# Product G's two outermost steps on half of the array's rows each, and where its results are read

## The chip, the cores and the metric

One core of one Trainium2 chip runs the whole program. The metric is the device time of one execution in microseconds (us).

## The reference, cut to what matters

Four layers, each `x = x + ffn(cond(x, style))` on x of 32 x 64 x 1024. `cond` is four modulated convolutions in a row over the 1024 positions of each of the 32 batches, with 64 channels in and out and 3 taps: the same length, up by 2 (transposed, then a blur), the same length, and a blur with a step down by 2.

```python
TYPES = ('same', 'upsample', 'same', 'downsample')
out = x
for i, typ in enumerate(TYPES):
    out = _layer(out, style, weights[i], biases[i], mod_w[i], mod_b[i], typ)
```

`_layer` scales the weights by the style of each batch, so each batch has weights of its own. `ffn` differs by layer: a product in fp8 (layer 0), a product with a low-rank top-2 of 16 experts (1), with 8 experts under a sparsemax (2), and a gated product of low rank (3).

## The kernel before, in words

The 32 batches are taken as 16 pairs (`NP` = 16). In a pair, h = 0 or 1 is the batch. A batch's 64 channels fill half of the 128 partitions, its even and odd positions the two halves, so a matmul has 128 rows. Every fp32 value is split in a high and a low part, and every product is three matmuls (`PASSES`: high by high, low by high, high by low).

Convolutions 2 to 4 of a batch are multiplied into one set of weights before they meet the data. For each pair there are, on TensorE (PE in the profile):

- `weights_a` (A, L796): 6 matmuls of 384 columns into bank 2. It waits for `gl_ready`, the reading of the pair before's product G from that bank.
- `weights_g` (G, L815): for each batch five steps e = -2 to 2 of three matmuls, 128 x 256 each, 30 in all. The window of 256 columns moves by 64 from step to step. Batch 0's result is in bank 2, batch 1's in bank 0. In the outermost steps half of the 128 rows have weights that are zero. `g_done` rises after each batch's 15 matmuls.
- `conv0` (L784): the first convolution, 12 matmuls of 512 columns into banks 0 and 1.
- `main` (L832): G's result by conv0's, 24 matmuls of 512 columns into banks 3 and 4.
- `transpose_h` (L841): 8 transposes of the result, into the same banks.
- `ffn` (L861, L877, L885 or L856), in layers 1 to 3 only. Layer 0's fp8 product is a stage of its own behind its 16 pairs.

Every engine has its order written out by hand, and semaphores tie them. ScalarE (ACT) reads a result from a bank and writes its high part, VectorE (DVE) reads it again and writes the low part: `read_u` (L968, L1124) for conv0, `read_g` (L973, L1130) for G, `read_a` (L962, L1118) for A, and `split_h` for the transposes. In layer 0 split_h is `H_all` on ACT (L989) and then `hmax`, a maximum over the pair, on DVE (L1141), whose end raises `hl_ready`. GpSimd (POOL) patches the edges of main's result before the transposes (L119).

`over_pairs` runs p = 0 (`first`), a loop over p = 1 to 12, and p = 13, 14, 15. `ahead` says how many pairs still follow. In iteration p, PE does A(p + 1), main(p), conv0(p + 1), transposes(p), G(p + 1), and in layers 1 to 3 ffn(p). So in layer 0, G(p + 1) is followed by A(p + 2) and main(p + 1), which open iteration p + 1.

```python
for h in range(2):
    pe.wait_ge(gl_ready, 2 * (g0 + p) + h + 1)
    pe.wait_ge(ul_ready, 2 * (g0 + p) + h + 1)
    if h == 0:
        wait_pos(pe, hh_ready, g0 + p)
        wait_pos(pe, hl_ready, g0 + p)
```

So main of a pair waits, before its first matmul, for its own G's low part (`gl_ready`) and for the split_h of the pair before (`hh_ready`, `hl_ready`), whose banks it writes again.

In p = 0 the order is another one, in all layers: A(1), edges_p, main(0), edges_v, conv0(1), edges_y, G(1), transposes(0), then ffn(0). The edge pass (`edges_u`, `edges_p`, `edges_v`, `edges_y`) computes the few positions at the ends of all batches. Its second product, `edges_p` (L743), has 64 rows: 9 matmuls of batch 0 on partitions 0 to 63, then 9 of batch 1 on partitions 64 to 127. Its results go through a long chain on DVE (L1178 to L1153) before `edges_v` (L756). G(0) stands ahead of p = 0.

## Time and profile before

| | |
|---|---|
| median of 3 runs | 2453.69 us (2453.54 to 2454.59) |
| the profiled execution | 2454.0 us, its span 2452.2 us |
| mean granted TensorE clock | 0.949 of full speed |
| PE busy | 2157.9 us, 88% |
| PE weight loads busy | 1796.4 us, 73% |
| DVE, ACT, POOL busy | 1093.3, 781.7, 447.8 us |
| G's matmuls (L815) | 1920, three groups of 640, 282 to 290 ns each |

The span is the time from the first to the last instruction of the profiled execution. Matmuls overlap, so one that lasts 0.28 us is followed by the next 0.12 us after its start; what a product takes is read from the starts.

### The profile page before, as it was taken

How to read it: one execution, taken by the hardware profiler on the slowest of the kernel's cores; microseconds unless marked ns; L12 is line 12 of the kernel's file. 1: busy time of each engine (PE TensorE's matmuls, PEld its weight loads, DVE VectorE, ACT ScalarE, POOL GpSimd, SP SyncE). 2: the span in 40 equal slices, each digit the busy share in tenths (PEclk: the TensorE clock that was granted, in tenths of full speed). 3: DMA queues.
4: the chain of work that ended last, by engine and by line, in shares of the span. 5: the costliest groups of instructions: out<-in, count | busy, mean ns of one | idle time of the engine just before them, and what ended most of it. 6: DMA issues, size and time to landing. Idle time of an engine off the chain costs nothing. (4 is left out here: it accounts for less than half of the span.)

```text
span 2452.2 us, 32019 instructions
## 1 busy us (share of the span) xinstructions
PE 2157.9 (88%) x10900; PEld 1796.4 (73%) x10900; DVE 1093.3 (45%) x1992; ACT 781.7 (32%) x1294; POOL 447.8 (18%) x478
## 2 busy tenths in 40 slices
PE   2799956679999995997599999997999979987997
PEld 2688832568888884886488888886888958866885
DVE  4656669634444433232443344435444424433442
ACT  2255621223323321011322232312454434423441
POOL 4021125320100110000411111111000012342334
PEclk9899989889999997998799999998999989998999
DMA  5333224322111203224211111102010021132123
GB/s 140 112 94 94 78 86 171 129 69 70 59 51 60 68 35 132 86 86 131 87 52 51 51 60 58 62 35 72 26 34 26 25 65 45 45 109 82 51 59 120
DMA packets 99008, 182.01 MB, mean 74 GB/s; under 512 B 21232, under 2 KB 50928, under 8 KB 98544
## 3 DMA queue, kind: packets, MB, share of 16 engines
q1 hardware_dynamic: 97680, 179.40, 23.2%
q10 hardware_dynamic: 1280, 1.97, 0.4%
q8 instruction: 30, 0.49, 0.1%
q14 instruction: 18, 0.15, 0.0%
HBM read 127.27 MB, written 46.92 MB: 71 GB/s over the span
## 5 line engine op out<-in xcount | busy, mean ns | idle before, releaser
L832 PE MATMUL ps<-l_u_hi,l_g_hi 128*128 128x512 f32 x512 | 205.1, 401 | 0.0
L832 PE MATMUL ps<-l_u_lo,l_g_hi 128*128 128x512 f32 x512 | 202.6, 396 | 0.0
L832 PE MATMUL ps<-l_u_hi,l_g_lo 128*128 128x512 f32 x512 | 202.6, 396 | 0.0
L1124 DVE TENSOR_TENSOR l_u_lo<-ps,l_u_hi 128x512 fp32r<-128x512 f32 x128 | 88.5, 693 | 222.3 <-ACT l_u_hi L968 222.2
L815 PE MATMUL ps<-l_a_hi,c_hi 128*128 128x256 f32 x640 | 185.8, 290 | 0.0
L815 PE MATMUL ps<-l_a_hi,c_lo 128*128 128x256 f32 x640 | 180.5, 282 | 0.0
L815 PE MATMUL ps<-l_a_lo,c_hi 128*128 128x256 f32 x640 | 180.3, 282 | 0.0
L119 POOL TENSOR_TENSOR l_hs<-l_EY,ones 128x4 f32<-128x4 f32 x128 | 28.2, 221 | 789.8 <-ACT l_hs L979 789.6
L877 PE MATMUL ps<-l_w_hi,l_h_hi 128*128 128x512 f32 x512 | 167.3, 408 | 0.0
L877 PE MATMUL ps<-l_w_lo,l_h_hi 128*128 128x512 f32 x512 | 163.4, 400 | 0.0
L877 PE MATMUL ps<-l_w_hi,l_h_lo 128*128 128x512 f32 x512 | 162.9, 399 | 0.0
L2047 POOL TENSOR_TENSOR f_a_lo<-f_prod,f_a_hi 128x512 fp32r<-128x512 f32 (+1 forms) x88 | 113.5, 1290 | 268.9 <-ACT f_a_hi L1950 268.9
L1874 PE MATMUL ps<-pt_hi,f_v_hi 128*128 128x512 f32 (+1 forms) x352 | 139.6, 397 | 25.3 <-DVE f_v_lo L1988 25.3
L784 PE MATMUL ps<-l_x_hi,c_hi 128*128 128x512 f32 x256 | 105.5, 412 | 63.1 <-DVE l_x_lo L1103 63.1
L979 ACT ACTIVATE l_hs<-ps,l_EY,dem3e 128x512 f32<-128x512 f32 x128 | 99.0, 777 | 156.0 <-PE ps L832 141.8
L2003 DVE SCALAR_TENSOR_TENSOR f_prod<-ps,f_b,f_gate 128x512 f32<-128x512 f32 (+1 forms) x88 | 66.0, 750 | 179.0 <-ACT f_gate L1943 179.0
L1874 PE MATMUL ps<-pt_lo,f_v_hi 128*128 128x512 f32 (+1 forms) x352 | 140.4, 399 | 0.0
L1874 PE MATMUL ps<-pt_hi,f_v_lo 128*128 128x512 f32 (+1 forms) x352 | 140.3, 398 | 0.0
L1130 DVE SCALAR_TENSOR_TENSOR l_g_lo<-ps,s_u,l_g_hi 128x512 fp32r<-128x512 f32 x128 | 95.8, 751 | 94.9 <-ACT l_g_hi L973 93.9
L962 ACT ACTIVATE l_a_hi<-ps,s_p 128x256 fp32r<-128x256 f32 x128 | 53.7, 470 | 252.6 <-PE ps L796 252.6
L973 ACT ACTIVATE l_g_hi<-ps,s_u 128x512 fp32r<-128x512 f32 x128 | 87.9, 688 | 122.7 <-PE ps L815 122.7
L968 ACT ACTIVATE l_u_hi<-ps 128x512 fp32r<-128x512 f32 x128 | 76.8, 600 | 143.2 <-PE ps L784 143.2
(303 smaller groups left out, 5073.8 us busy)
## 6 DMA issues: line engine op xcount, KB each, us to landing
xin<-x SPq DMA_DIRECT2D x96, 256.0 KB, 4.0
l_xr<-x SPq DMA_DIRECT2D x32, 512.0 KB, 4.5
x<-l_xr SPq DMA_DIRECT2D x32, 512.0 KB, 2.7
l_stage<-in_ffn_w SPq DMA_DIRECT2D x24, 512.0 KB, 3.3
f_v<-in_ffn_v SPq DMA_DIRECT2D x84, 128.0 KB, 2.7
xnat<-in_x SPq DMA_DIRECT2D x16, 512.0 KB, 3.5
xin<-xpl SPq DMA_DIRECT2D x64, 128.0 KB, 2.9
q_xr<-in_x SPq DMA_DIRECT2D x16, 512.0 KB, 3.8
```

The lines of the kernel that those rows point to most:

```text
L784: mm = nc.tensor.matmul(ps[:, h, :], c_part[ws][:, B0 + t * P:B0 + (t + 1) * P], Xs[ms][:, h, t:t + HALF], start=(k == 0), stop=(k == 5))
L815: mm = nc.tensor.matmul(ps[:, bank, at:at + 4 * C], c_part[ws][:, UT + at:UT + at + P], As[ms][:, h, :], start=(k == 0), stop=(k == 14), s ...
L832: mm = nc.tensor.matmul(ps[:, 3 + h, :], Gs[ws][:, h, at:at + P], Us[ms][:, h, 1 + q:1 + q + HALF], start=(k == 0), stop=(k == 11))
L877: mm = nc.tensor.matmul(ps[:, 5 + o, :], hsp[ws][:, b, :], wsp[ms][:, b, o * HALF:(o + 1) * HALF], start=(k == 0), stop=(layer == 1 and k ...
L968: nc.scalar.activation(Us[0][:, h, 1:HALF + 1], ps[:, h, :], ACT.Copy).then_inc(uh_ready, 1)
L973: nc.scalar.activation(Gs[0][:, h, :], ps[:, 2 if h == 0 else 0, :], ACT.Copy, scale=column(s_u, p, h)).then_inc(gh_ready, 1)
L979: nc.scalar.activation(hs[:, h, :], ps[:, 3 + h, :], ACT.Identity, bias=EY[:, 1, 0, bass.ds(h * NP + p, 1)], scale=dem3e[:, bass.ds(h * NP ...
L1124: v.tensor_tensor(Us[1][:, h, 1:HALF + 1], ps[:, h, :], Us[0][:, h, 1:HALF + 1].bitcast(F32), ALU.subtract).then_inc(ul_ready, 1)
L1130: v.scalar_tensor_tensor(Gs[1][:, h, :], ps[:, 2 if h == 0 else 0, :], column(s_u, p, h), Gs[0][:, h, :].bitcast(F32), ALU.mult, ALU.subtr ...
L1874: mm = nc.tensor.matmul(ps[0:m, 2 * g + gu, :], v1sp[ws][:, s, r, gu, 0:m], pt[ms][:, r, cols], start=(k == 0), stop=(k == 5))
L2003: v.scalar_tensor_tensor(prod[0:m, g, :], ps[0:m, 2 * g + 1, :], b1[0:m, 1, bass.ds(2 * i + g, 1)], gate[0:m, g, :], ALU.add, ALU.mult).th ...
L2047: nc.gpsimd.tensor_tensor(asp[1][0:m, g, :], prod[0:m, g, :], asp[0][0:m, g, :].bitcast(F32), ALU.subtract).then_inc(al_ready, 1)
```

## The change

G's 30 matmuls become 18 whole ones (128 rows, the steps e = 1, 0 and -1 of both batches) and 12 with 64 rows (`ends`). The 64-row ones go in pairs: a step of one batch on partitions 0 to 63 and one of the other batch on 64 to 127, which write different banks. The order is now: 6 whole of batch 0, 6 whole of batch 1, 6 halves, 6 whole, a wait for `ends_done`, 6 halves. `g_done` rises by 2 at the very end, where it rose by 1 after each batch. The wait for `ul_ready` stands behind 6 matmuls, where it stood behind 15.

`edges_p` issues its two batches' 64-row matmuls in turn.

In layer 0, and there alone, G(p + 1) stands before the transposes of p on PE, and read_g before split_h on ACT and DVE. In layers 1 to 3 that order stays.

The remaining edits rename semaphores: `side` is shared by layers 1 to 3 with an offset `side0`, and `ends_done` is new. They add or remove no instruction.

```diff
@@ PE: edges_p, the edge pass's second product
-                for h in range(2):
-                    rows = slice(h * C, h * C + C)
-                    k = 0
-                    for t in range(TAPS):
-                        for ws, ms in PASSES:
+                k = 0
+                for t in range(TAPS):
+                    for ws, ms in PASSES:
+                        for h in range(2):
+                            rows = slice(h * C, h * C + C)
                             mm = nc.tensor.matmul(
                                 ps[:, 5 + h, 0:NP * 3 * PW].rearrange("p (n k) -> p n k", k=PW),
                                 c_part[ws][rows, CU + t * P:CU + (t + 1) * P], UEs[ms][rows, :, t:t + PW],
                                 start=(k == 0), stop=(k == 8))
-                            k += 1
+                        k += 1
@@ PE: weights_g, product G
-                for h in range(2):
-                    if h == 0:
-                        pe.wait_ge(al_ready, 2 * (g0 + p) + 2)
-                    else:
-                        pe.wait_ge(ul_ready, 2 * (g0 + p) + 1)
-                    bank = 2 if h == 0 else 0
-                    k = 0
-                    for e in range(-2, 3):
-                        at = (2 - e) * C
-                        for ws, ms in PASSES:
-                            mm = nc.tensor.matmul(ps[:, bank, at:at + 4 * C],
-                                                  c_part[ws][:, UT + at:UT + at + P], As[ms][:, h, :],
-                                                  start=(k == 0), stop=(k == 14), skip_group_check=True)
-                            k += 1
-                    mm.then_inc(g_done, 1)
+                pe.wait_ge(al_ready, 2 * (g0 + p) + 2)
+
+                def window(h, e, rows, ws, ms, **flags):
+                    at = (2 - e) * C
+                    return nc.tensor.matmul(ps[:, 2 if h == 0 else 0, at:at + 4 * C],
+                                            c_part[ws][rows, UT + at:UT + at + P], As[ms][rows, h, :],
+                                            skip_group_check=True, **flags)
+
+                def whole(h, e):
+                    for k, (ws, ms) in enumerate(PASSES):
+                        window(h, e, slice(0, P), ws, ms, start=(e == 1 and k == 0), stop=False)
+
+                def ends(pairs):
+                    for ws, ms in PASSES:
+                        for h, e, rows in pairs:
+                            mm = window(h, e, rows, ws, ms, start=False, stop=(pairs is last_ends and ws == 1))
+                    return mm
+
+                first, second = slice(0, C), slice(C, P)
+                first_ends, last_ends = ((0, 2, first), (1, -2, second)), ((0, -2, second), (1, 2, first))
+                whole(0, 1)
+                whole(0, 0)
+                pe.wait_ge(ul_ready, 2 * (g0 + p) + 1)
+                whole(1, 1)
+                whole(1, 0)
+                ends(first_ends).then_inc(ends_done, 1)
+                whole(0, -1)
+                whole(1, -1)
+                pe.wait_ge(ends_done, g0 + p + 1)
+                ends(last_ends).then_inc(g_done, 2)
@@ PE: iteration
                 main(p)
                 if ahead:
                     conv0(p + 1)
+                if layer == 0 and ahead:
+                    weights_g(p + 1)
                 transpose_h(p)
-                if ahead:
-                    weights_g(p + 1)
                 if layer > 0:
+                    if ahead:
+                        weights_g(p + 1)
                     ffn(p)
@@ ACT and DVE: iteration, the same edit on both
                 if ahead:
                     read_u(p + 1)
+                    if layer == 0:
+                        read_g(p + 1)
                 split_h(p)
-                if ahead:
+                if ahead and layer > 0:
                     read_g(p + 1)
```

What PE issues in a late iteration of layer 0, before. L784 is conv0, L841 a transpose, L815 G, L796 A, ident and l_hs the operands of a transpose, gl_ready the low part of G.

```order
L841 MATMUL ps<-ident,l_hs 128x128 [waits hs_patched]
L841 MATMUL ps<-ident,l_hs 128x128 x3
L841 MATMUL ps<-ident,l_hs 128x128 [waits hs_patched]
L841 MATMUL ps<-ident,l_hs 128x128 x3
L815 MATMUL ps<-l_a_hi,c_hi 128x256 [waits al_ready]
L815 MATMUL ps<-l_a_lo,c_hi 128x256
L815 MATMUL ps<-l_a_hi,c_lo 128x256
```

The same place of the change, the end of G and what follows it up to the first matmul of A. L814 is G, L861 a transpose, L798 A.

```order
L814 MATMUL ps<-l_a_hi,c_hi 128x256 [waits ends_done]
L814 MATMUL ps<-l_a_hi,c_hi 128x256
L814 MATMUL ps<-l_a_lo,c_hi 128x256 x2
L814 MATMUL ps<-l_a_hi,c_lo 128x256 x2
L861 MATMUL ps<-ident,l_hs 128x128 [waits hs_patched]
L861 MATMUL ps<-ident,l_hs 128x128 x3
L861 MATMUL ps<-ident,l_hs 128x128 [waits hs_patched]
L861 MATMUL ps<-ident,l_hs 128x128 x3
L798 MATMUL ps<-l_z_hi,c_hi 128x2x192 [waits gl_ready,zl_ready]
```

The transposes moved from ahead of G to between G and A; the six halves at G's end are each other's neighbours in pairs.

What DVE issues in the same iteration of layer 0, before: l_u_lo is read_u's low part, l_g_lo read_g's, l_a_lo read_a's of the next iteration.

```order
L1124 TENSOR_TENSOR l_u_lo<-ps,l_u_hi 128x512 [waits uh_ready] x2
L1141 TENSOR_REDUCE hmax<-l_hs 128x1 [waits hs_patched,hh_ready]
L1130 SCALAR_TENSOR_TENSOR l_g_lo<-ps,s_u,l_g_hi 128x512 [waits gh_ready] x2
L1118 SCALAR_TENSOR_TENSOR l_a_lo<-ps,s_p,l_a_hi 128x256 [waits ah_ready]
L1118 SCALAR_TENSOR_TENSOR l_a_lo<-ps,s_p,l_a_hi 128x256
```

And now:

```order
L1148 TENSOR_TENSOR l_u_lo<-ps,l_u_hi 128x512 [waits uh_ready] x2
L1154 SCALAR_TENSOR_TENSOR l_g_lo<-ps,s_u,l_g_hi 128x512 [waits gh_ready] x2
L1165 TENSOR_REDUCE hmax<-l_hs 128x1 [waits hs_patched,hh_ready]
L1142 SCALAR_TENSOR_TENSOR l_a_lo<-ps,s_p,l_a_hi 128x256 [waits ah_ready]
L1142 SCALAR_TENSOR_TENSOR l_a_lo<-ps,s_p,l_a_hi 128x256
```

hmax moved behind the two readings of G; on ACT, H_all moved behind its two readings in the same way.

## Rows read from the trace of the kernel before

**Rows 1.** Busy time by stretch: stretch, length, busy PE, PEld, DVE, ACT, POOL, clock.
```profile
142.50:327.00 184.50, 179.85 (x1027) 156.43 (x1025) 117.00 (x191) 106.76 (x175) 29.21 (x37) 1.00 0.28 80
1239.00:1620.00 381.00, 381.00 (x2014) 325.09 (x2014) 158.25 (x409) 111.06 (x190) 44.02 (x70) 1.00 0.17 57
```

**Rows 2.** Timeline, PE, one iteration of layer 0: start, us, engine, line, operation, idle before.
```profile
184.24 1.03 PE L841 MATMUL ps<-ident,l_hs 128*128 128x128 f32 x8
...
185.23 0.28 PE L815 MATMUL ps<-l_a_lo,c_hi 128*128 128x256 f32 x1
...
188.54 0.28 PE L815 MATMUL ps<-l_a_hi,c_lo 128*128 128x256 f32 x1
188.79 0.44 PE L796 MATMUL ps<-l_z_hi,c_hi 128*128 128x384 f32 x1
...
189.94 0.39 PE L832 MATMUL ps<-l_u_hi,l_g_hi 128*128 128x512 f32 x1
...
198.34 0.60 PE L841 MATMUL ps<-ident,l_hs 128*128 128x128 f32 x4
```

**Rows 3.** Timeline, PE, into and out of 64-row matmuls, edges_p of layer 0.
```profile
76.65 0.34 PE L796 MATMUL ps<-l_z_hi,c_lo 128*128 128x384 f32 x1
...
76.92 0.43 PE L743 MATMUL ps<-l_ue_hi,c_hi 64*128 64x288 f32 x1
...
77.18 0.33 PE L743 MATMUL ps<-l_ue_lo,c_hi 64*128 64x288 f32 x1
...
77.87 0.34 PE L743 MATMUL ps<-l_ue_hi,c_lo 64*128 64x288 f32 x1
...
77.88 0.51 PE L743 MATMUL ps<-l_ue_hi,c_hi 64*128 64x288 f32 x2
...
79.36 0.34 PE L743 MATMUL ps<-l_ue_hi,c_lo 64*128 64x288 f32 x1
...
79.63 0.50 PE L832 MATMUL ps<-l_u_hi,l_g_hi 128*128 128x512 f32 x1
...
79.97 0.40 PE L832 MATMUL ps<-l_u_lo,l_g_hi 128*128 128x512 f32 x1
```

**Rows 4.** Timeline, PE, into 64-row matmuls inside one product of layer 3's ffn stage.
```profile
2174.43 0.39 PE L1888 MATMUL ps<-f_a_hi,f_u_lo 128*128 128x512 f32 x1
2174.75 0.50 PE L1888 MATMUL ps<-f_a_hi,f_u_hi 64*128 64x512 f32 x1
2175.09 0.39 PE L1888 MATMUL ps<-f_a_lo,f_u_hi 64*128 64x512 f32 x1
```

**Rows 5.** Timeline, ACT and DVE, the iteration of rows 2, and two readings of G in a row (layer 2).
```profile
185.41 1.03 ACT L989 ACTIVATE H_all<-ps 128x1024 f32 x1 [0.37 <-PE ps L841]
...
186.68 1.22 DVE L1141 TENSOR_REDUCE hmax<-l_hs 128x1024 f32 x1 [0.91 <-ACT H_all L989]
...
187.98 0.75 DVE L1130 SCALAR_TENSOR_TENSOR l_g_lo<-ps,s_u,l_g_hi 128x512 fp32r<-128x512 f32 x1
...
188.95 0.69 ACT L973 ACTIVATE l_g_hi<-ps,s_u 128x512 fp32r<-128x512 f32 x1 [1.09 <-PE ps L815]
...
189.76 0.75 DVE L1130 SCALAR_TENSOR_TENSOR l_g_lo<-ps,s_u,l_g_hi 128x512 fp32r<-128x512 f32 x1 [1.02 <-ACT l_g_hi L973]
...
1205.71 1.26 ACT L973 ACTIVATE l_g_hi<-ps,s_u 128x512 fp32r<-128x512 f32 x2
```

**Rows 6.** Timeline, PE, iteration p = 1 of layer 0: its transposes and the next main.
```profile
126.44 1.97 PE L841 MATMUL ps<-ident,l_hs 128*128 128x128 f32 x8 [3.76 <-POOL l_hs L119]
...
133.53 0.39 PE L832 MATMUL ps<-l_u_hi,l_g_hi 128*128 128x512 f32 x1
```

**Rows 7.** Timeline, ACT, between G(0) and the reading of A(1) in layer 2.
```profile
1172.28 1.05 ACT L995 ACTIVATE l_w_hi<-l_stage 128x1024 fp32r<-128x1024 f32 x1
```

**Rows 8.** Timeline, DVE and PE, layer 2: the gated values, and the transpose that uses them.
```profile
1258.92 0.29 DVE L1286 TENSOR_TENSOR l_hg<-l_small,l_gate 128x128 f32<-128x128 f32 x1
...
1263.71 0.27 PE L873 MATMUL ps<-ident,l_hg 128*128 128x128 f32 x1
```

More of the change, by code:

```diff
@@ L607, in conv_phase @@
         g_done, gh_ready, gl_ready = sem("g_done"), sem("gh_ready"), sem("gl_ready")
+        ends_done = sem("ends_done")
         m_done, hs_ready, hs_patched = sem("m_done"), sem("hs_ready"), sem("hs_patched")
@@ L614, in conv_phase @@
         chunk_loaded = [sem(lay + f"chunk_loaded{s}") for s in range(2)]
-        side = [sem(lay + f"side{i}") for i in range(5 if layer < 3 else 4)]
+        side = [sem(f"side{i}" if layer else f"l0_side{i}") for i in range(5)]
+        side0 = [NP * k for k in ((0, 0, 0, 0), (0, 0, 0, 0), (1, 1, 0, 0), (2, 2, 1, 1))[layer]]
         if layer == 0:
@@ L850, in ffn @@
                 if layer == 3 and not first:
-                    pe.wait_ge(side[3], p)
+                    pe.wait_ge(side[3], side0[3] + p)
                 k = 0
@@ L871, in ffn @@
                     if layer == 2 and b == 6:
-                        pe.wait_ge(side[0], p + 1)
+                        pe.wait_ge(side[0], side0[0] + p + 1)
                         nc.tensor.transpose(ps[:, 7, 3 * P:4 * P], hg[:, :, :].rearrange("p e r -> p (e r)"),
@@ L881, in ffn @@
                 if layer == 2:
-                    pe.wait_ge(side[3], p + 1)
+                    pe.wait_ge(side[3], side0[3] + p + 1)
                     for k, (ws, ms) in enumerate(PASSES):
@@ L890, in transpose_p @@
             def transpose_p(p):
-                pe.wait_ge(side[0], p + 1)
+                pe.wait_ge(side[0], side0[0] + p + 1)
                 for r in range(2):
@@ L998, in tail @@
                 if layer == 1:
-                    act.wait_ge(side[0], p + 1)
+                    act.wait_ge(side[0], side0[0] + p + 1)
                     nc.scalar.activation(ex[:, :], small[:, R1:R1 + E1], ACT.Exp, bias=nmax[:, :],
@@ L1002, in tail @@
                 if layer == 2:
-                    act.wait_ge(side[1], p + 1)
+                    act.wait_ge(side[1], side0[1] + p + 1)
                     nc.scalar.activation(gsp[0][:, :], ps[:, 7, 3 * P:4 * P], ACT.Copy).then_inc(side[2], 1)
@@ L1009, in tail_p @@
             def tail_p(p):
-                act.wait_ge(side[1], p + 1)
+                act.wait_ge(side[1], side0[1] + p + 1)
                 nc.scalar.activation(kept["pt_hi"][:, :, bass.ds(p * P, P)],
@@ L1242, in tail @@
                     v.tensor_scalar(nmax[:, :], top[:, 0:1], -1.0, None, ALU.mult).then_inc(side[0], 1)
-                    dve.wait_ge(side[1], p + 1)
+                    dve.wait_ge(side[1], side0[1] + p + 1)
                     link(3, v.reciprocal(den[:, 0:1], esum[:, :]))
@@ L1300, in tail_p @@
             def tail_p(p):
-                dve.wait_ge(side[2], p + 1)
+                dve.wait_ge(side[2], side0[2] + p + 1)
                 cols = bass.ds(p * P, P)
@@ L1310, in _ @@
             if layer in (1, 2):
-                dve.wait_ge(side[4], 16 * layer)
+                dve.wait_ge(side[4], 8 * layer * (layer + 1))
             def quantise(i):
@@ L1367, in iteration @@
                     read_u(p + 1)
+                    if layer == 0:
+                        read_g(p + 1)
                 split_h(p)
-                if ahead:
+                if ahead and layer > 0:
                     read_g(p + 1)
```

4 lines of the change are left out of this document (2 added, 2 removed).

## The prediction

> **What bounds the kernel now.** I read the busy time by stretch first. In layer 0's loop TensorE is busy 179.85 of 184.50 us, in layer 2's 381.00 of 381.00, at full clock [rows 1]. So in the loops a matmul slot saved or added is time saved or added, and so is every wait that opens on TensorE. ACT and DVE are under two thirds busy there: they matter by how late they hand something over. Then the timeline of one iteration of layer 0. From its transposes at 184.24 to the next ones at 198.34 are 14.10 us. From transposes to the next main it is 189.94 - 184.24 = **5.70 us**, and from main to the next transposes 8.40 us: 36 matmuls of 512 columns, 0.233 us each [rows 2]. G's matmuls start (188.54 - 185.23) / 28 = **0.118 us** apart [rows 2]: a slot. 2453.69 us is the median of the runs; the profiled execution, against which the sum is made, took 2454.0, 0.3 more.
>
> **1. G's slots.** 30 slots become 18 whole and, if the two batches' halves run side by side, 6 for the 12 halves: 24. That they do run so can be seen in edges_p. The first matmul of the second batch starts at 77.88, as the sixth of the first batch does at 77.87, each line going on at its own pace; the row with x2 is two that overlap [rows 3]. Six slots less are 6 x 0.118 = 0.71 us per pair.
>
> **2. Going between whole and half.** This is what the 0.71 us pays. Entering L743, the second matmul starts 77.18 - 76.92 = 0.26 after the first, where the later ones keep (77.87 - 77.18) / 4 = 0.172: 0.09 lost; the first had itself come 0.27 after the last whole one. Leaving, the gaps are 0.27 in place of 0.172 and 79.97 - 79.63 = 0.34 in place of 0.233: 0.10 + 0.11 [rows 3]. Inside one product, with no other batch of work or result awaited, the same: 0.32 and 0.34 in place of 0.233, 0.09 + 0.11 [rows 4]. A changeover thus costs about 0.19 to 0.20 us, in two halves: the loads of weights start only when the array has run out, and the first load is not hidden. I take **0.19**. G now has four (into the halves, out, in, out): 0.76 us against 0.71 saved, so **+0.05 us per pair**. For the load that is not hidden the Trainium skill gives a figure ("TensorE: Matmul & The Clock Gate", LDWEIGHTS): columns / 1.2, so 107 ns for 128 columns, where the rows leave 90 to 110. By 107 in all four the sum would be some 0.03 us more per pair, 1 to 2 us in all. The bounds for a changeover go from 0 (the load hides) to 0.20. The wait for ends_done costs nothing: six whole matmuls (0.71 us) stand between, longer than the 0.28 a matmul takes to end, and the changeover empties the array there anyway. A changeover into a product that is waiting costs nothing either.
>
> In layers 1 to 3, 14 iterations each, G stands in a full TensorE: 42 x 0.05 = **+2.1 us**. G's results come later there, both at the end, but ffn follows on TensorE: in layer 3 24 matmuls of 256 columns, 2.8 us, before A, in layers 1 and 2 far more. On DVE the readings end some 0.6 us later and push the router's chain back; its last value is written at 1258.92 + 0.29 = 1259.21 and used at 1263.71 [rows 8], so 4.5 us cover that.
>
> **3. Layer 0: who waits for the reading of G.** Here nothing but A follows G, and the edit changes three things: both readings start at G's very end, hmax stands behind them on DVE, H_all behind them on ACT, and main waits for hmax by hl_ready. Time is counted from the end of conv0's slots (184.24 in rows 2).
> - G starts at once. Its last matmul starts after 23 slots and three changeovers: 2.71 + 0.57 = 3.28.
> - It ends 0.28 later, and ACT starts 0.13 after that (188.54 + 0.28 = 188.82, then 188.95) [rows 2, 5]: 3.69.
> - ACT's second reading starts 1.26 - 0.69 = 0.57 after the first [rows 5], and H_all another 0.57 later: 4.83. The transposes, 1.03 us [rows 2], run meanwhile and are just done.
> - H_all takes 1.03; hmax starts 0.24 after its end (186.44, 186.68) and takes 1.22 [rows 5]: 7.32.
> - TensorE starts 0.06 after DVE's end (187.98 + 0.75 = 188.73, A at 188.79) [rows 2, 5]: main starts at **7.38**.
>
> Before it was 5.70. So each such iteration is **1.68 us** longer. Before, H_all and hmax were hidden beside G's matmuls; that cover is gone. A is not what decides: it waits for the first low part, at 3.69 + 0.69 + 0.12 + 0.75 + 0.06 = 5.31, and takes 189.94 - 188.79 = 1.15, so main could start at 6.46. Iterations p = 2 to 14 have all this: 13 x 1.68 = **+21.8 us**.
>
> p = 1 is another case. There TensorE idles 3.76 us before its transposes, for POOL; they start at 126.44 and main at 133.53, 7.09 later [rows 6]. G (about 3.6 us) now falls into that idle time, and from the transposes to main remain 1.03 + 0.13 + 1.03 + 0.24 + 1.22 + 0.06 = 3.71: **-3.4 us**.
>
> **4. Each layer's first pair.** G(0) is followed by A(1) and A(1) by the chain that ends in edges_v. A(1) now waits for a reading that starts at G's end. A started 0.25 after G's last matmul, now 5.31 - 3.28 = 2.03 after one that starts 0.23 earlier (28 x 0.118 + 0.20 against 3.28): **+1.6 us** in layer 0. In layers 1 to 3 ACT has two chunks of weights to split between G(0) and read_a, 1.05 us each [rows 7], so most of that is covered: 0.5 each, between 0 and 1.6, **+1.5 us**. edges_p itself becomes shorter by about 1 us, which brings nothing: DVE's chain behind it, not edges_p, says when edges_v starts.
>
> **Sum.** 2.1 + 21.8 - 3.4 + 1.6 + 1.5 = +23.6 us. 2454.0 + 23.6 = 2477.6, less the 0.3 for the median: **2477.3 us**, 1.0% slower. Unknown sizes (changeovers 0.17 to 0.20, the chain of part 3 by 0.2 us each, first pairs) give 2470 to 2486 as this case's own range.
>
> **Rivals.**
> - **The halves don't run side by side**, the change doesn't do what it says. 6 slots more, in 42 + 13 pairs: 55 x 0.71 = 39, so 2516 us. Against it stand the two rows at 77.87 and 77.88; for it only that there the overlap lasted for four matmuls, and that here two loads must fit in 0.118.
> - **Changeovers are free** where the next load is ready: the other side. Then 0.76 is gained in 42 iterations and 0.57 in 13, 39 us: 2438, faster by 0.6%. It decides from 0.05 us per changeover down (there 2448.8, the bound of faster). Against it are three places with 0.19 to 0.20, none with less. The Trainium skill ("TensorEngine Tiling (Array Packing)", Theoretical Speedup) promises up to 2x for 64 rows, which taken alone is this rival; under Key Properties the same page of the Trainium skill says that a change of tiling mode drains TensorE.
> - **hmax doesn't decide in layer 0**, A does: main at 6.46, +0.76 in 13 iterations, 9.9 in place of 21.8: 2465. For it: hmax reads no bank, so nothing but the wait itself holds main. Against it: the wait is in the code, before main's first matmul, and hmax now starts after both readings of G.
> - **The clock falls in layer 0.** TensorE would idle some 1.6 us in each iteration, in two pieces with A between. At p = 1 the eight transposes took 1.97 in place of 1.03 after an idle time [rows 2, 6], at the lower of the two levels (1.2 GHz). 0.94 later transposes push H_all and hmax by about as much: 13 x 0.9 = 12, 2489 us, more if main's beginning falls too. Against it: these idle pieces are much shorter than the 3.76 us.
>
> **Chances and range.** Forecast 0.65, not side by side 0.06, free changeovers 0.07, A decides 0.09, clock 0.08, anything else 0.05. A measurement of this kernel tells 0.2%, 5 us, from no change. Faster by more: 0.09; within: 0.03; slower by more: 0.88. The range takes in the forecast's own, "A decides" and the clock case: **2462 to 2497 us**.
>
> **What would show it.** In layer 0's loop an iteration of about 15.8 us in place of 14.1; TensorE idle before main, released by hmax, about 0.9 us each, and before A, released by the low part of G; H_all and hmax behind the two readings. In G: the halves in pairs that start within 0.01 us, 0.118 from pair to pair, and gaps of about 0.21 at each of four changeovers. In layers 1 to 3 an iteration as long as before within 0.1 us. The prediction is wrong if layer 0's iteration is no longer than 14.5 us, or if G in layers 1 to 3 takes less than 3.3 us or over 4.

## The result and the profile after

| | before | changed kernel |
|---|---|---|
| median of 4 runs each, on the same chip | 2454.14 us (2453.54 to 2454.73) | 2484.57 us (2483.13 to 2487.91) |
| ratio | | 1.0126, 95% interval 1.0108 to 1.0143 |
| span of the profiled execution | 2452.2 us | 2482.0 us |
| mean granted TensorE clock | 0.949 | 0.946 |

The changed kernel is 30.4 us slower; 23.6 were forecast. From the profile's costliest groups (busy time and mean of one | idle time before, and what ended it):

```profile
L852 PE MATMUL ps<-l_u_hi,l_g_hi 128*128 128x512 f32 x512 | 206.6, 404 | 13.4 <-DVE hmax L1165 13.4
...
L814 PE MATMUL ps<-l_a_hi,c_hi 128*128 128x256 f32 (+1 forms) x640 | 168.8, 340 | 0.0
...
L814 PE MATMUL ps<-l_a_lo,c_hi 128*128 128x256 f32 (+1 forms) x640 | 144.6, 281 | 0.0
```

L852 is main (L832 before), L814 is G (L815 before). Main, which had waited for nothing that the profile shows, now waits 13.4 us in all for hmax. The busy time by stretch, for the stretches of [rows 1]:

```profile
142.50:327.00 184.50, 165.82 (x925) 134.80 (x924) 102.53 (x169) 94.71 (x160) 29.04 (x33) 0.99 0.27 78
```

In layer 0 TensorE is busy for 165.8 us of the same 184.5 us, not 179.9, with 925 matmuls for 1027: the loop is slower because TensorE stands idle, not because its work grew. One iteration of layer 0, TensorE, which answers to [rows 2]:

```profile
142.33 0.28 PE L814 MATMUL ps<-l_a_hi,c_hi 128*128 128x256 f32 x1
...
145.64 0.28 PE L814 MATMUL ps<-l_a_hi,c_lo 64*128 64x256 f32 x2
145.85 1.09 PE L861 MATMUL ps<-ident,l_hs 128*128 128x128 f32 x8
147.67 0.44 PE L798 MATMUL ps<-l_z_hi,c_hi 128*128 128x384 f32 x1 [0.72 <-DVE l_g_lo L1154]
...
149.84 0.47 PE L852 MATMUL ps<-l_u_hi,l_g_hi 128*128 128x512 f32 x1 [0.84 <-DVE hmax L1165]
150.15 0.40 PE L852 MATMUL ps<-l_u_lo,l_g_hi 128*128 128x512 f32 x1
```

and ACT and DVE beside it, which answer to [rows 5]:

```profile
146.05 1.26 ACT L995 ACTIVATE l_g_hi<-ps,s_u 128x512 fp32r<-128x512 f32 x2 [2.92 <-PE ps L814]
147.21 1.02 ACT L1011 ACTIVATE H_all<-ps 128x1024 f32 x1
```

```profile
148.47 1.22 DVE L1165 TENSOR_REDUCE hmax<-l_hs 128x1024 f32 x1 [0.20 <-ACT H_all L1011]
```

This is the chain that the prediction wrote down: G's last start 3.31 after its first (3.28 predicted), both readings, H_all, hmax, and main at 149.84 - 142.33 = 7.51 (7.38 predicted; 5.70 before). Now G in layer 2, where TensorE is full:

```profile
1279.52 0.28 PE L814 MATMUL ps<-l_a_hi,c_lo 128*128 128x256 f32 x1
1279.73 0.39 PE L814 MATMUL ps<-l_a_hi,c_hi 64*128 64x256 f32 x2
1279.95 0.29 PE L814 MATMUL ps<-l_a_lo,c_hi 64*128 64x256 f32 x2
1280.07 0.28 PE L814 MATMUL ps<-l_a_hi,c_lo 64*128 64x256 f32 x2
1280.28 0.39 PE L814 MATMUL ps<-l_a_hi,c_hi 128*128 128x256 f32 x1
1280.51 0.28 PE L814 MATMUL ps<-l_a_lo,c_hi 128*128 128x256 f32 x1
```

Each x2 is two halves, 3 ns apart in the trace: they run side by side, 0.12 from pair to pair. A changeover shows as two gaps. The first matmul of the other kind comes 0.21 after the last one in place of 0.118, and the second one 0.22 to 0.23 after the first: 0.09 + 0.10. Main's starts in layer 2, one row of each kernel for p = 2 and one for p = 14, give the iteration: before (1610.98 - 1269.06) / 12 = 28.493 us, changed kernel (1640.22 - 1297.50) / 12 = 28.560.

```profile
1269.06 0.40 PE L832 MATMUL ps<-l_u_hi,l_g_hi 128*128 128x512 f32 x1
...
1610.98 0.40 PE L832 MATMUL ps<-l_u_hi,l_g_hi 128*128 128x512 f32 x1
```

```profile
1297.50 0.40 PE L852 MATMUL ps<-l_u_hi,l_g_hi 128*128 128x512 f32 x1
...
1640.22 0.40 PE L852 MATMUL ps<-l_u_hi,l_g_hi 128*128 128x512 f32 x1
```

Subtracting the start of each main before from the same one after, for all 64, shows where the 30 us come from:

| stretch of the program | predicted | trace |
|---|---|---|
| up to main(2) of layer 0, with p = 1 | 1.6 - 3.4 = -1.8 | +0.3 |
| layer 0, main(2) to main(15) | +21.8 | +26.9 |
| layers 1 to 3, first pairs and what lies between layers | +1.5 | +1.4 |
| layers 1 to 3, main(1) to main(15) | +2.1 | +2.3 |
| behind the last main | 0 | -1.1 |

The sum of the right column is 29.8, the difference of the two spans.

Rows two and four stand on iterations that repeat; rows one and three don't. In the traces of the five kernels below that have the old G and the old order in layer 0, main(2) starts anywhere from 133.5 to 136.0 us, and in the four kernels that have the changed kernel's code in layers 1 to 3 (the changed kernel itself among them) the third row lies between -2.0 and +5.9. That +1.4 meets +1.5 there is luck.

### The profile page after: what moved, and what is told of

The parts are those of the page before. It is cut to its first block and busy times, and to the rows that moved or that the text cites. A ratio compares the mean times of both kernels' runs of the same rounds, so it can differ in the third digit from the quotient of the medians.

```text
span 2482.0 us, 32127 instructions
## 1 busy us (share of the span) xinstructions
PE 2169.0 (87%) x10900; PEld 1768.7 (71%) x10900; DVE 1084.9 (44%) x1992; ACT 774.8 (31%) x1294; POOL 448.1 (18%) x478
## 5 line engine op out<-in xcount | busy, mean ns | idle before, releaser
L852 PE MATMUL ps<-l_u_hi,l_g_hi 128*128 128x512 f32 x512 | 206.6, 404 | 13.4 <-DVE hmax L1165 13.4
L852 PE MATMUL ps<-l_u_lo,l_g_hi 128*128 128x512 f32 x512 | 203.3, 397 | 0.0
L852 PE MATMUL ps<-l_u_hi,l_g_lo 128*128 128x512 f32 x512 | 203.1, 397 | 0.0
L814 PE MATMUL ps<-l_a_hi,c_hi 128*128 128x256 f32 (+1 forms) x640 | 168.8, 340 | 0.0
L1154 DVE SCALAR_TENSOR_TENSOR l_g_lo<-ps,s_u,l_g_hi 128x512 fp32r<-128x512 f32 x128 | 90.2, 746 | 149.4 <-ACT l_g_hi L995 149.4
L814 PE MATMUL ps<-l_a_lo,c_hi 128*128 128x256 f32 (+1 forms) x640 | 144.6, 281 | 0.0
L814 PE MATMUL ps<-l_a_hi,c_lo 128*128 128x256 f32 (+1 forms) x640 | 144.1, 280 | 0.0
L995 ACT ACTIVATE l_g_hi<-ps,s_u 128x512 fp32r<-128x512 f32 x128 | 81.0, 684 | 165.1 <-PE ps L814 165.1
L852 PEld LDWEIGHTS ps<-l_u_hi,l_g_hi 128*128 128x128 f32 x512 | 97.7, 191 | 38.9 <-issue 18.6
```

What stands on the lines that cost most here:

```text
L814: return nc.tensor.matmul(ps[:, 2 if h == 0 else 0, at:at + 4 * C], c_part[ws][rows, UT + at:UT + at + P], As[ms][rows, h, :], skip_group_ ...
L852: mm = nc.tensor.matmul(ps[:, 3 + h, :], Gs[ws][:, h, at:at + P], Us[ms][:, h, 1 + q:1 + q + HALF], start=(k == 0), stop=(k == 11))
L995: nc.scalar.activation(Gs[0][:, h, :], ps[:, 2 if h == 0 else 0, :], ACT.Copy, scale=column(s_u, p, h)).then_inc(gh_ready, 1)
L1154: v.scalar_tensor_tensor(Gs[1][:, h, :], ps[:, 2 if h == 0 else 0, :], column(s_u, p, h), Gs[0][:, h, :].bitcast(F32), ALU.mult, ALU.subtr ...
```

## Experiments

All iterations below are from start to start of main between p = 2 and p = 14, taken from each kernel's trace as above:

| kernel | median of runs (before beside it) | ratio, 95% interval | layer 0 | layer 1 | layer 2 | layer 3 |
|---|---|---|---|---|---|---|
| before | 2454.14 | | 14.10 | 26.873 | 28.493 | 16.993 |
| changed kernel | 2484.57 (2454.14) | 1.0126 (1.0108 to 1.0143) | 16.10 | 26.941 | 28.560 | 17.023 |
| G's ends whole | 2490.55 (2456.16) | 1.0150 (1.0122 to 1.0177) | 16.33 | 26.872 | 28.493 | 16.953 |
| old order, new G | 2504.44 (2456.16) | 1.0193 (1.0167 to 1.0219) | 17.03 | 26.941 | 28.560 | 17.025 |
| new order, old G | 2475.06 (2456.16) | 1.0079 (1.0055 to 1.0103) | 15.81 | 26.873 | 28.493 | 16.993 |
| main free of hmax | 2468.67 (2456.16) | 1.0051 (1.0036 to 1.0066) | 14.90 | 26.941 | 28.560 | 17.050 |
| change in layers 1 to 3 only | 2459.29 (2455.18) | 1.0015 (1.0005 to 1.0025) | 14.10 | 26.941 | 28.560 | 17.050 |
| one block of halves | 2482.32 (2455.18) | 1.0105 (1.0088 to 1.0122) | 15.90 | 26.877 | 28.493 | 16.980 |
| edge pass only | 2456.24 (2455.18) | 1.0004 (0.9995 to 1.0014) | 14.10 | 26.872 | 28.493 | 16.993 |
| two signals | 2464.00 (2455.18) | 1.0036 (1.0023 to 1.0048) | 14.83 | 26.865 | 28.492 | 16.982 |
| covered block | 2428.94 (2455.69) | 0.9883 (0.9866 to 0.9899) | 14.10 | 26.280 | 27.894 | 16.396 |
| six changeovers | 2476.35 (2455.69) | 1.0082 (1.0065 to 1.0099) | 14.10 | 27.319 | 28.943 | 17.433 |
| covered block in layer 0 too | 2432.08 (2455.02) | 0.9902 (0.9885 to 0.9918) | 14.24 | 26.292 | 27.907 | 16.400 |

Each kernel is compared with the times of the kernel before that were taken beside it; where two changed kernels lie closer than their intervals, the iterations tell them apart and not the totals. In the expectations R1 is "the halves don't run side by side", R2 "changeovers are free", R3 "hmax doesn't decide". R5 is a rival that the prediction didn't have: that the single signal at G's end costs, whatever the order.

### What do a half and a changeover cost?

The first kernel makes G's ends whole again. The other half's weights are zero, so the sums stay the same:

```diff
-                first, second = slice(0, C), slice(C, P)
+                first = second = slice(0, P)
```

> The changed kernel, but the four half-row groups of each G are made over all 128 rows again (both names stand for the whole range of rows), so that no matmul runs beside another and TensorE's rows never change between whole and half; order, banks, waits and semaphores stay the changed kernel's. It leaves out nothing but computes other sums at the ends. Theory on record: 30 slots of 0.118 us for 24, +0.71, against four changeovers of 0.19, -0.76, so G gets shorter by about 0.05 us a pair: G in layer 2 about 3.5 to 3.6 us, the time 2 to 4 us under the changed kernel's 2484.6, near 2482. If the changeovers were free (rival R2), G would get longer by 0.71 and the time some 30 to 39 us longer than the changed kernel's. If the halves did not run side by side (rival R1), G would get shorter by over 0.7 us and the time 30 to 39 us shorter.

The price came out, the total didn't. In layers 1 and 2 the iteration is 0.067 to 0.069 us shorter than the changed kernel's, and as long as before, to 1 ns. So 6 slots of 0.118 stand against four changeovers c: 4c = 0.71 + 0.067, c = **0.194**. R1 and R2 both fall. The total rose where I expected -2 to -4: by 6 us in the medians, by 4 if each is taken against the kernel before beside it, and by 2.4 in the span of the profiled execution. The intervals of the two ratios overlap, and the four runs of this kernel lie 9.5 us apart, so the size is not known. That it didn't fall has a reason in layer 0, which I had taken as unmoved: there only three of the changeovers lie before G's last start, and 29 slots (3.42 us) are longer than 23 slots and three changeovers (3.28), so the chain behind G starts later, and each iteration at full clock is 0.1 longer (16.1 for 16.0); and the granted clock was 0.50 for 3.4 us at 212.8 and again at 294.8, one time more than in the changed kernel's loop.

The second counts changeovers the other way. One of the first group's three pairs is cut off by a whole step; layer 0 is as before:

```diff
-                ends(first_ends).then_inc(ends_done, 1)
+                ends(first_ends, PASSES[:1])
                 whole(0, -1)
+                ends(first_ends, PASSES[1:]).then_inc(ends_done, 1)
                 whole(1, -1)
```

> Layer 0 as before, the new G in layers 1 to 3, but with one of the first group's three pairs of halves cut off by a whole step: six changeovers between whole and half rows for each G in place of four, with the same matmuls. Theory on record (0.19 us each): the pair grows by 0.39 over that kernel's, so by 0.45 over the kernel before in layer 2, in all +17 us over the 2459 of the kernel with the new G in layers 1 to 3 alone: about 2475. If the price is one of the new G as a whole and not of each changeover, the time stays near 2459.

As expected: against the kernel with the change in layers 1 to 3 only, layer 2 takes 28.943 - 28.560 = 0.383 more for two changeovers, **0.19** each, with the same matmuls. The price belongs to each change of rows.

The third takes two changeovers away by putting the two groups side by side, with the wait bare between them:

```diff
-                ends(first_ends).then_inc(ends_done, 1)
                 whole(0, -1)
                 whole(1, -1)
+                ends(first_ends).then_inc(ends_done, 1)
                 pe.wait_ge(ends_done, g0 + p + 1)
                 ends(last_ends).then_inc(g_done, 2)
```

> The changed kernel with both groups of halves adjacent at G's end, so that TensorE changes between whole and half rows twice for each G in place of four times; the wait for the first group then stands bare between the two groups. Theory on record (0.19 us a changeover): two changeovers less, -0.39 us, and in their place the bare wait: from the first group's last start to the next group's first start about 0.4 us in place of 0.12, +0.29 (a matmul of G is on record for 0.28 us and a wait for an end costs some 0.1 more). Together -0.1 us a pair, 55 pairs: 3 to 8 us under the changed kernel, 2477 to 2482, and in layer 2 the pair -0.03 against the kernel before. If what I call a changeover costs nothing and the new G is long for another reason (rival), the pair grows by 0.29, +16 us.

```profile
1278.35 0.39 PE L814 MATMUL ps<-l_a_hi,c_hi 64*128 64x256 f32 x2
1278.57 0.29 PE L814 MATMUL ps<-l_a_lo,c_hi 64*128 64x256 f32 x2
1278.69 0.28 PE L814 MATMUL ps<-l_a_hi,c_lo 64*128 64x256 f32 x2
1279.04 0.39 PE L814 MATMUL ps<-l_a_hi,c_hi 64*128 64x256 f32 x2
1279.26 0.28 PE L814 MATMUL ps<-l_a_lo,c_hi 64*128 64x256 f32 x2
```

The wait shows between 1278.69 and 1279.04: 0.34 in place of 0.118, and the load behind it is not hidden either, 0.22 to the next. A bare wait is thus 0.33 us, not the 0.29 that I had, and -0.71 + 0.39 + 0.33 = 0.01: the iteration is back at 28.493. The total is 2.3 us under the changed kernel, a little less than the 3 to 8 that I gave, and the intervals of the two overlap. What the block would give without the wait was not tried: its two groups write the same banks from different rows.

### What costs 1.9 us in layer 0?

New order, old G (the kernel before with these lines, and the same move of `read_g` on ACT and DVE):

```diff
+                if layer == 0 and ahead:
+                    weights_g(p + 1)
                 transpose_h(p)
-                if ahead:
-                    weights_g(p + 1)
                 if layer > 0:
+                    if ahead:
+                        weights_g(p + 1)
                     ffn(p)
```

> The kernel before with layer 0's new order alone; the old G, its signal after each batch, and the edge pass stay. Theory on record (the order puts H's transposes, reads and hmax behind G, and main waits for hmax): +1.6 to +1.9 us for each of 13 iterations, less 3.4 at p=1, so +18 to +22 us: 2472 to 2477 us, with an idle time of some 0.9 us before main that hmax ends. Rival R5 (the single signal at G's end is what costs, whatever the order): within 3 us of 2454.1.

The order alone: 15.81 - 14.10 = +1.71 us an iteration, 19 us in all, as expected. The wait is in the profile's lines, larger than in the changed kernel, since here batch 0's part is read during G, A follows the transposes at once, and all the waiting falls before main (in that kernel main is L832 and hmax L1145):

```profile
L832 PE MATMUL ps<-l_u_hi,l_g_hi 128*128 128x512 f32 x512 | 206.9, 404 | 24.7 <-DVE hmax L1145 24.7
```

One of these waits; in the iterations p = 2 to 12 they are all 1.71 us, in one piece, and the granted clock stays at 1.00 throughout layer 0's loop:

```profile
210.07 0.47 PE L832 MATMUL ps<-l_u_hi,l_g_hi 128*128 128x512 f32 x1 [1.71 <-DVE hmax L1145]
```

New order, new G, but main doesn't wait for hmax:

```diff
-                        wait_pos(pe, hl_ready, g0 + p)
+                        if layer > 0:
+                            wait_pos(pe, hl_ready, g0 + p)
...
             def read_h(p):
+                if layer == 0:
+                    wait_pos(act, hl_ready, g0 + p)
```

> The changed kernel, but in layer 0 TensorE's main no longer waits for hmax; the wait for it stands on ScalarE ahead of its read of main's result, so that everything stays ordered. Theory on record (rival R3's arithmetic, with hmax out of the way): main then starts when A's operands and G's are in, about 6.5 us after the end of conv0's slots in place of 7.5: -0.9 to -1.1 us for each of 13 iterations, 12 to 14 us shorter than 2484.6, near 2472; the idle time that hmax ends goes from 13 us to about nothing, and what main waits for next is G's last read. If ScalarE's later read turns into the same wait (it has nothing else to do meanwhile), the time stays within 3 us of 2484.6.

The iteration is 14.90, 0.80 over before where rival R3 had worked out 0.76. That is 1.1 us shorter than the changed kernel's iteration, 16.0 at full clock (its mean of 16.10 has one fall of the clock in it). The time fell by 16 us, 2 more than given; the clock's fall inside layer 0's loop went too. So hmax was what main waited for. A is next, and not G's last read, as I had written: A still waits 0.72 us for the first low part, and main follows it without a gap.

Old order, new G, where my expectation failed (the edit is against the changed kernel; `read_g` also stands behind `split_h` again):

```diff
-                if layer == 0 and ahead:
-                    weights_g(p + 1)
                 transpose_h(p)
+                if ahead:
+                    weights_g(p + 1)
                 if layer > 0:
-                    if ahead:
-                        weights_g(p + 1)
                     ffn(p)
```

> The changed kernel with layer 0's queues in the old order again (on TensorE G behind the transposes, on ScalarE and VectorE G's reads behind those of H); the new G stays. Theory on record, in which TensorE's next main waits for hmax: the transposes come before G now, so H is read and hmax ends while G runs; the wait for hmax goes and one for G's last read (g_hi and g_lo behind H on their engines) takes its place, as in the kernel before. Main should start about as early after conv0 as before plus the 0.05 us that G itself got longer: about 5.75 to 5.9 us after the end of conv0's slots, 1.6 to 1.8 us earlier than in the changed kernel, times 13, less the 3.4 us that the new order gains at p=1: 18 to 20 us shorter than 2484.6, near 2465. But the new G signals both of its batches only at its end, where the old one signalled the first batch half way, and its reads (1.2 us for the first, behind H) then come in one go: if that decides (rival R5), main starts 7.3 to 7.5 us after conv0, as late as in the changed kernel, and the time is 0 to 5 us from 2484.6.

20 us slower than the changed kernel, not 20 faster. TensorE, one iteration:

```profile
185.28 0.28 PE L814 MATMUL ps<-l_a_hi,c_lo 64*128 64x256 f32 x2
187.31 0.44 PE L798 MATMUL ps<-l_z_hi,c_hi 128*128 128x384 f32 x1 [1.75 <-DVE l_g_lo L1150]
187.59 0.34 PE L798 MATMUL ps<-l_z_lo,c_hi 128*128 128x384 f32 x1
187.76 0.34 PE L798 MATMUL ps<-l_z_hi,c_lo 128*128 128x384 f32 x1
187.94 0.42 PE L798 MATMUL ps<-l_z_hi,c_hi 128*128 128x384 f32 x1
188.16 0.52 PE L798 MATMUL ps<-l_z_lo,c_hi 128*128 128x384 f32 x1
...
188.79 0.63 PE L852 MATMUL ps<-l_u_hi,l_g_hi 128*128 128x512 f32 x1
```

Nothing is left between G's end and A to cover G's first reading: A waits 1.75 us for the first low part, because the new G signals both batches at its end, where the old one had signalled batch 0 after 15 slots. The two iterations at full clock are 1.78 and 1.82 us longer than before, and so 0.1 shorter than the changed kernel's: that is rival R5 of the expectation. In the others a stretch at half the clock, 1.2 GHz, comes with the idle time (busy time by stretch; behind POOL's column stands the granted clock):

```profile
174.40:188.10 13.70, 11.95 (x72) 9.98 (x71) 7.22 (x12) 5.63 (x8) 2.39 (x3) 1.00 0.29 96
188.10:191.50 3.40, 3.40 (x11) 2.83 (x10) 1.38 (x3) 2.35 (x6) 0.00 (x0) 0.50 0.00 0
```

Here the fall comes 0.8 us after A's start. There are ten such falls of 3.4 us in the twelve iterations from p = 2 on, between 0.3 us before A's start and 1.0 us after it. One that lies wholly in an iteration costs about another 1.6 us: eight of the iterations are 3.2 to 3.5 us longer than before. Why the clock falls here is open. The kernel with the order alone has 1.71 us of idle time in one piece in each iteration, against 1.75 here, and no fall. So the order alone costs 1.71 us and the signal alone 1.8 at full clock, **and not in sum**: the changed kernel, with both, is 1.89 over before. Its order covers part of G's reading by the transposes, and A stands between the two waits that are left, 0.72 and 0.84 us.

The test of that: old order, the group of ends first, then batch 0's whole steps with a signal and batch 1's with another:

```diff
                 pe.wait_ge(ul_ready, 2 * (g0 + p) + 1)
...
                 ends(first_ends).then_inc(ends_done, 1)
...
                 pe.wait_ge(ends_done, g0 + p + 1)
-                ends(last_ends).then_inc(g_done, 2)
+                ends(last_ends)
+                for h in range(2):
+                    for e in (1, 0, -1):
+                        mm = whole(h, e)
+                    mm.then_inc(g_done, 1)
```

> The new G with its halves first (first group, bare wait, second group), then batch 0's whole steps and a signal, then batch 1's and a second signal; layer 0's old order; in all layers. Written after the old order with the changed kernel's G had cost more than the new order (2504 us): the thought is that layer 0 pays for either of two things, the order or the single signal at G's end, each about 1.8 us an iteration and not in sum. With two signals in the old order the first reads of G start some 0.7 us later than before in place of 1.6 or more, so layer 0 +0.7 for each of 13 iterations, about +9; layers 1 to 3 -0.03 for 42 pairs, first pairs -1 to +2: 2460 to 2465 us. If the single signal is not the cause, layer 0 stays 1.8 us an iteration over before: 2478 or more.

14.83 us, +0.73 where I expected +0.7, 2464.0 us, and no fall of the clock in the loop. With an earlier first reading 1.1 of the 1.8 us go: the late first reading is the cause.

### The rest of the change

The changed kernel with layer 0 as before (the old G's code and the old order):

```diff
             def weights_g(p):
+                if layer == 0:
+                    for h in range(2):
...
+                        mm.then_inc(g_done, 1)
+                    return
```

> Layer 0 entirely as before (old G with its two signals, old order), the new G and the interleaved edge pass in layers 1 to 3. Theory on record: +0.05 us for each of 42 later pairs (+2.1; the changed kernel's own trace shows +0.07 in layers 1 and 2 and +0.03 in layer 3, so +2.6), first pairs 0 to +1.5: +2 to +4 us over the kernel before, about 2457 if that one is at 2454. Rival (a part of the 30 us comes from the new G in the later layers by way of something the pairs' starts do not show): over +8.

+0.068, +0.067 and +0.057 us a pair, +4 us in all (between 1 and 6 by the interval; the later pairs give 2.7): the new G by itself is a small loss, and nearly all of the 30 us is layer 0.

The kernel before with the edge pass alone:

```diff
-                for h in range(2):
...
+                for t in range(TAPS):
+                    for ws, ms in PASSES:
+                        for h in range(2):
```

> The kernel before with the edge pass interleaved alone. On record: the edge pass lies beside the DVE chain that the first pairs wait for, so 0 to -1 us over the four layers, same as the kernel before within 0.1%. If it were on the path, 9 slots less four times would be up to -4 us.

No difference that the runs can tell. The interleaved edge pass does start its matmuls as nine pairs and ends 0.9 us earlier, but `edges_v` waits for DVE's `l_pe_lo` in both kernels and starts 10.08 us after edges_p's first matmul in both (76.92 and 87.00 before, 76.96 and 87.04 here).

### A version faster than both

If a changeover costs 0.19 and a bare wait 0.33, G's halves pay only with two changeovers and no bare wait. Work of the same kind must stand between the two groups. The transposes of H can be it: they write other banks, and half a transpose's rows make half of its columns. The kernel has, in layers 1 to 3 from p = 1 on (layer 0 as before):

```diff
+                def turn(swap):
+                    for k in range(4):
+                        for h in range(2):
+                            rows = second if h != swap else first
+                            at = k * P + rows.start
+                            mm = nc.tensor.transpose(ps[:, 3 + h, at:at + C], hs[rows, h, k * P:(k + 1) * P],
+                                                     ident[rows, rows])
+                    return mm
...
+                    turn(0).then_inc(t_half, 1)
...
+                ends(first_ends, turned).then_inc(ends_done, 1)
...
+                    turn(1).then_inc(t_done, 1)
+                pe.wait_ge(ends_done, g0 - NP + p + 1)
+                ends(last_ends)
```

and then the whole steps with two signals. The wait for `t_half` stands ahead of the first group's third pair, the one for H's edges ahead of conv0's last matmul.

> Layer 0 as before. In layers 1 to 3, from the third pair on, one stretch of half rows for each pair: H's eight transposes are made as sixteen halves, eight beside eight (batch 0's first rows beside batch 1's last, then the other way round), with G's first group of ends between the two and the second group behind them; then batch 0's whole steps and a signal, batch 1's and a signal. Two changeovers for each pair in place of the changed kernel's four, and the waits between the groups lie behind the other groups. Theory on record (6 slots of 0.118 saved, 0.19 a changeover): -0.71 + 0.39 = -0.32 us a pair, less up to 0.15 for one wait that has only two slots to hide behind: -0.17 to -0.32 for each of 42 pairs, -7 to -13 us, first pairs 0 to +4: 2442 to 2451 us beside 2454 to 2455 for the kernel before, so faster than both kernels. If half transposes take longer than whole ones, or are not made side by side, up to +0.4 a pair on top, and no gain.

```profile
1244.27 0.39 PE L788 MATMUL ps<-l_x_hi,c_lo 128*128 128x512 f32 x1
1244.59 0.46 PE L855 MATMUL ps<-ident,l_hs 64*128 64x64 f32 x8
1244.86 0.36 PE L831 MATMUL ps<-l_a_hi,c_hi 64*128 64x256 f32 x2
1245.06 0.28 PE L831 MATMUL ps<-l_a_lo,c_hi 64*128 64x256 f32 x2
1245.18 0.32 PE L831 MATMUL ps<-l_a_hi,c_lo 64*128 64x256 f32 x2
1245.34 0.41 PE L855 MATMUL ps<-ident,l_hs 64*128 64x64 f32 x8
1245.57 0.39 PE L831 MATMUL ps<-l_a_hi,c_hi 64*128 64x256 f32 x2
```

2428.9 us: 1.2% faster than the kernel before and 2.2% faster than the changed one. -0.60 us a pair, twice what I expected. What I had missed: I gave the halved transposes the time of whole ones. In the trace the pairs of halves start 0.059 apart, whole transposes 0.109 (the rows of x8 above are four pairs each, and what follows starts 0.27 and 0.23 later). Eight steps of 0.109 against eight of 0.059 are 0.40 us. With the -0.32 and some 0.1 for the waits and the loads behind them (1245.18 to 1245.34 is 0.16, and 0.20 to 0.22 follows the first of each group) that makes about the 0.60. It is a sum from the starts: no kernel has the block without the halved transposes, so how the gain splits between them is worked out and not measured.

Is TensorE's time worth the same in layer 0? The block for all layers, against the kernel just shown (the other places that had set layer 0 apart change with it):

```diff
-                if layer > 0 and ahead:
+                if ahead:
                     weights_g(p + 1, p)
```

> The same stretch of halves of transposes and G, now in layer 0 as well. TensorE's work falls by 0.60 us for each pair there too (as measured in layers 1 to 3). Theory: in layer 0 that is worth nothing, because the iteration is set by the chain from batch 0's signal: the signal comes (in the kernel with the block in layers 1 to 3) 2.6 us after the first transpose's start, as before (8 slots of 0.11 and 15 of 0.118: 2.64); but the transposes end 0.17 later, and hmax, ahead of G's first low part on VectorE, ends 0.17 later, so A starts up to 0.17 later: 0 to +0.17 for each of 13 iterations, TensorE idle some 0.7 us before A, and the time 0 to 4 us over the 2429 of the block in layers 1 to 3 alone. If slots were worth their length in layer 0 too (rival), 13 x 0.6 = 8 us less: 2421.

No. TensorE has 0.5 us less to do there (14.25 us with 0.69 of them idle, in place of 14.10 with none), and the iteration is 0.15 us longer:

```profile
178.19 0.39 PE L867 MATMUL ps<-l_u_hi,l_g_hi 128*128 128x512 f32 x1
...
186.67 0.46 PE L838 MATMUL ps<-ident,l_hs 64*128 64x64 f32 x8
...
189.24 1.22 DVE L1177 TENSOR_REDUCE hmax<-l_hs 128x1024 f32 x1 [1.13 <-ACT H_all L1025]
189.66 0.69 ACT L1009 ACTIVATE l_g_hi<-ps,s_u 128x512 fp32r<-128x512 f32 x1 [0.66 <-PE ps L814]
190.47 0.75 DVE L1166 SCALAR_TENSOR_TENSOR l_g_lo<-ps,s_u,l_g_hi 128x512 fp32r<-128x512 f32 x1
191.28 0.44 PE L800 MATMUL ps<-l_z_hi,c_hi 128*128 128x384 f32 x1 [0.69 <-DVE l_g_lo L1166]
...
192.44 0.39 PE L867 MATMUL ps<-l_u_hi,l_g_hi 128*128 128x512 f32 x1
```

From main to the transposes are 8.48 us in place of 8.40, since the way into the transposes is now a changeover (0.32 from conv0's last matmul to them in place of 0.233); from the transposes to main are 5.77 in place of 5.70. Of these 0.07, 0.06 come with batch 0's signal: ACT starts to read 2.99 us after the first transpose in place of 2.93. I had put it down to hmax, which stands ahead of the low part on DVE, and the low part does start 0.01 after hmax ends (190.46). But it also starts 0.12 after the high part ends (190.35), and it does so in the kernel before:

```profile
187.17 0.69 ACT L973 ACTIVATE l_g_hi<-ps,s_u 128x512 fp32r<-128x512 f32 x1 [0.73 <-PE ps L815]
```

(187.86 and 187.98 [rows 5]). The two are ready together, and the trace doesn't show that hmax adds anything. What decides is the chain from batch 0's signal to A. At 179.85 of 184.50 us busy [rows 1] layer 0 looked bound by TensorE; but A started 0.25 after G's last matmul [rows 2], 0.13 later than a slot would have it, 0.06 after the low part's end. The chain was already the longer of the two, by 0.13 us.

## Why the prediction was right, and where it was off

The sign, the size (30.4 us measured, 23.6 forecast, 2484.6 inside 2462 to 2497) and the mechanism hold. Layer 0's loop, the largest term, came out 5 us too small, in three parts that are told below; the first pairs' term was met by luck.

- **Step 1, the halves side by side:** shown by the pairs 3 ns apart and by the kernel with whole ends.
- **Step 2, 0.19 us a changeover and +0.05 a pair:** 0.194 from one kernel, 0.19 from the next, +0.067 in layers 1 and 2 and +0.03 in layer 3 (+0.057 there in two of the other kernels; why layer 3 differs is open). 42 pairs: +2.3 for +2.1. The Trainium skill's 107 ns for the load that is not hidden ("TensorE: Matmul & The Clock Gate", LDWEIGHTS), which by the prediction's estimate would have made it 0.03 us more per pair, agrees with the gaps of 0.22 to 0.23, which are 0.10 to 0.11 over 0.118.
- **The rival of free changeovers:** each costs 0.19. The Trainium skill's up to 2x for 64 rows ("TensorEngine Tiling (Array Packing)", Theoretical Speedup) holds for the slots, 12 halves in 6; what the same page of the Trainium skill says under Key Properties, that a change of tiling mode drains TensorE, is the other half of the matter; what the traces show of it is the 0.21 in place of 0.118 at each changeover.
- **Step 3, main waits for hmax, +1.68 us an iteration:** the chain is as written, and taking hmax off main moved it to where A decides. The term was undersized by 0.21. **What was missing is TensorE's restart:** I had main 0.06 after DVE's end, from a row where an A of 384 columns restarts; main starts 0.15 after hmax (148.47 + 1.22 = 149.69, then 149.84), which with 0.04 from smaller terms makes the 7.51, and its second matmul comes 0.31 after the first in place of 0.233 (150.15), so that conv0 ends 8.48 after main's start and not 8.40. 12 times 0.21 is 2.5 us. A does restart 0.06 after the low part in the changed kernel too; why main takes longer is open.
- **The last iteration** of layer 0 (main(14) to main(15)) is 2.9 us longer, not 1.7: 1.2 us. Before it had been 12.8 us long and not 14.1, because no A follows G(15): main(15) starts 0.12 after G's last matmul. In the changed kernel leaving A out saves nothing, since main waits for hmax. I had taken this iteration like the others.

```profile
315.37 0.28 PE L815 MATMUL ps<-l_a_hi,c_lo 128*128 128x256 f32 x1
315.49 0.45 PE L832 MATMUL ps<-l_u_hi,l_g_hi 128*128 128x512 f32 x1
```

```profile
342.68 0.47 PE L852 MATMUL ps<-l_u_hi,l_g_hi 128*128 128x512 f32 x1 [2.60 <-DVE hmax L1165]
```

- **The clock:** it fell once within layer 0's loop, at 246.1, for 3.4 us: that iteration was 3.4 us longer in place of 1.9. I had that as a rival for every iteration or none; it came in one. In the kernel with the old order it came ten times.
- **p = 1, -3.4:** -2.0 between these two traces. G did fall into the idle time. But the transposes come 0.75 us later after main(1) than before, with POOL's work on the planes, which they wait for there (124.34 before, 127.45 now, while main(1) is 2.4 later); and from them to main are 4.30 us and not 3.71, 0.49 of it because the transposes take 1.52, in part at a granted clock of 0.50. A single pair of traces doesn't fix this term: main(1) to main(2) takes 20.3 to 22.8 us in the five kernels with layer 0's old G and old order and 17.1 to 18.6 in the five with the new order, 3.2 apart in the mean.
- **What I should have seen** is that the reading of G had two covers, the early signal and the place of the transposes. The prediction names both edits (readings at G's very end, H behind them) and works out main through hmax (7.38) and through A (6.46), but it treats hmax's new place as the cause of the whole loss. Each edit alone costs nearly all of it. It was right in sum since the dearer of the two ways decides.

## To carry to other kernels

Splitting a matmul over half of the rows pays by the slot but costs about 0.19 us here for each change between whole and half, so collect all half-row work (transposes too) in one stretch, and let pieces on other banks cover its waits. Before work is taken from an engine that looks full, follow each signal it gives: one that comes later or after another reader can cost more than the saved slots, and two delays that hide each other don't add up, so undoing one of them may bring nothing: here it made the kernel slower.

## What the hardware showed that I had not expected

- Half transposes (64 rows, 64 columns) start 0.059 us apart as pairs, whole ones 0.109: sixteen halves side by side take little more than half the time of eight whole ones.
- A wait on TensorE for its own result costs 0.34 us from start to start in place of 0.118, and 0.10 more since the next load is not hidden.
- Idle times of about the same length did different things to the clock in layer 0's loop: 1.75 us in one piece ahead of A came with ten falls of the granted clock to 0.50 in twelve iterations, 1.71 us in one piece ahead of main with none, and 0.72 and 0.84 us with A between with one. Neither the sum nor the length of a piece tells which; what does was not found.
